# Relation stage: loop over pairs of groups, source-row fills spread over the groups, second bias moved into the relation table

## The chip, the core and the metric

One core of one Trainium2 chip runs the kernel. The metric is the device time of one execution in microseconds. Engines are named as the profile names them: PE (TensorE matmul), PEld (its weight loads), DVE (VectorE), ACT (ScalarE), POOL (GpSimd) and SP (SyncE).

## The reference

Four graph layers run over the same 25,000 edges of a graph with 100,000 nodes of 32 features, each with a residual and a layer norm. The third layer is the one that the change touches:

```python
x = h[src]; y = h[dst]; c = w_comp[etype]
xb = jnp.einsum('ei,bio->ebo', x, weight)          # 16 bases
msg = jnp.einsum('eb,ebo->eo', c, xb)
x_hat = x @ A1_w.T + A1_b
y_hat = y @ A2_w.T + A2_b + rel_emb[etype]
a = jnp.tanh(jax.nn.relu(jnp.sum(x_hat * y_hat, axis=-1) / scale))
nei = segment_sum(a[:, None] * msg, dst)
curr = h[src[last_e]] @ self_loop_weight
h_new = relu(where(in_deg > 0, nei + curr, 0))
```

After it, every node row goes through the last two norms. Rows of nodes that are only sources are written to the output while the relation layer is still being computed, because they get nothing from it.

## The kernel before

The edges lie as 128 partitions by 196 columns (T), so one column is 128 edges. The relation stage takes them in 49 groups (NG) of four columns (GT). Groups are gathered in 7 rounds (ROUNDS) of 7 groups (RG). All engines but SP and POOL walk through the same 49 groups, each in its own program, tied by semaphores. Each group has one of two buffers, b. In the kernel before, b is j % 2, where j is the group's number within its round (0 to 6). So group 6 of a round and group 0 of the next have the same buffer.

For a group g the work is:

- ACT, `stage` (L2262 to L2271): copies the source rows as two half-precision parts (L2268) and the target rows (L2271) into a staging buffer. It does so for group g + 1 ahead of the rest of group g.
- PE, `relation_transpose` (L2559, L2561): transposes group g + 1, into PSUM. In PE's queue this stands ahead of the products of group g.
- ACT: copies group g's transposes out of PSUM (L2321 and L2322), waits until DVE has used group g's linear terms (L2323), and copies the self-loop terms out (L2325).
- PE: the linear products (L2571, L2573, L2575), then the products with the 16 bases, four of 512 columns (L2580), two for each pair of PSUM banks.
- DVE, `relation_groups` (L1988): y_hat plus relation row (L2014), the first two columns' products times the basis weights (L2003, into `prods`), x_hat times y_hat (L2018), the other two columns (L2003, into `nx`), then three sums (L2009, L2025, L2009) and a scale with relu (L2031). Once a round it adds the second bias to the relation rows of that round's 28 columns (L1990).

The rows of plain source nodes leave through a ring of two slots. A slot holds 14 columns (U). ACT scales each column into the slot by an activation (L2332) and copies the 14 indices (L2334). POOL then sends the 14 columns, each by one indirect DMA to the output (`out_src_slot`, L834, L839). ACT fills slots 0 and 1 ahead of the first group, and two more at the end of each of the first six rounds (`out_src_round`, L2336), after waiting for the landing of the slot's earlier contents.

`free(g, j)` gives the count at which a double buffer may be written again. For j = 0 it asks for one group more than elsewhere, because the neighbour has the same buffer. `groups` runs six rounds as a loop, and the last round without a loop.

After the stage DVE multiplies by the tanh, sums over segments and hands a table to SP for writing; POOL then fetches rows of this table (L719, L724).

Of the kernel before, what the change touches and what calls it, by code (L numbers as in the profile page):

```python
# [68 lines left out]
def gnn_resnorm(nc, x, src, dst, etype, eweight, w1, fc_w, fc_b, bias1, w2, w_comp, w_self, A1w, A1b, A2w, A2b,  # L69
# [53 lines left out]
    with ctx:  # L123
# [376 lines left out]

        def free(g, j):


            return g + (CREDIT if j == 0 else CREDIT - 1)

        def groups(eng, body, round_end=None):

            with eng.Fori(0, ROUNDS - 1) as i:
                for j in range(RG):
                    body(i * RG + j, j, False)  # L510
                if round_end:
                    round_end(i)
            for j in range(RG):
                body((ROUNDS - 1) * RG + j, j, j == RG - 1)

# [149 lines left out]
        def _(pool):  # L665
# [167 lines left out]

            def out_src_slot(n, b):  # L834

                pool.wait_ge(s_oslot, n + 1)
                pool.sem_inc(s_tick[0], 1)
                for t in range(U):
                    pool.indirect_dma_start(out=out[:, :], out_offset=bass.IndirectOffsetOnAxis(  # L839
                        ap=oidx[:, b, t:t + 1], axis=0), in_=oring[b][:, t * D:(t + 1) * D], in_offset=None,  # L840
                        bounds_check=N - 1, oob_is_err=False).then_inc(s_oland[b], 16)


            pool.wait_ge(s_nout, 16 * CH)
            with pool.Fori(0, ROUNDS) as k:
                for b in range(2):
                    out_src_slot(k * 2 + b, b)
            pool.wait_ge(s_tabw, 32)
# [8 lines left out]
            for b in range(2):  # L857
                pool.wait_ge(s_oland[b], 16 * U * ROUNDS)
            for h in range(2):
# [6 lines left out]
        def mid(ap, n):  # L866

            return ap.unsqueeze(1).to_broadcast([ap.shape[0], n, ap.shape[1]])

        @block.vector  # L870
        def _(dve):
# [815 lines left out]
            for j in range(GT):  # L1687
# [15 lines left out]
                st.do(V.tensor_copy(bdy[r, j * D:(j + 1) * D], aw[r, D:2 * D]))  # L1703

            st.seq(V.tensor_copy(rel3[:, 0, :], relf[:, :]))
            for k in range(2):
# [280 lines left out]

            def relation_groups(i):  # L1988
                rel = chunk(RB, i, RW)[:, :, NB:RW]
                st.seq(V.tensor_tensor(rel, rel, mid(b_b2[:, :], RC), ALU.add))  # L1990
                pr3 = pr2[:, :].rearrange("p (t o) -> p t o", t=GT)
                pq3 = pq2[:, :].rearrange("p (t o) -> p t o", t=GT)
                for j in range(RG):
                    g, b = i * RG + j, j % 2
                    xh = bank[6 + b][:, 0:256].rearrange("p (t o) -> p t o", t=GT)
                    yh = bank[6 + b][:, 256:256 + P].rearrange("p (t o) -> p t o", t=GT)
                    relg = RB[:, bass.ds(g * (GT * RW), GT * RW)].rearrange("p (t o) -> p t o", t=GT)

                    def basis_mult(c):

                        dve.wait_ge(s_msg, g * GT + (2 * c + 2 + MSG0))
                        dve.sem_inc(tick, 1)
                        st.do(V.tensor_tensor(wide_prods[c].rearrange("p (t o b) -> p t o b", t=2, b=NB),  # L2003
                                              pairs[c][:, :].rearrange("p (t o b) -> p t o b", t=2, b=NB),
                                              relg[:, 2 * c:2 * c + 2, 0:NB].unsqueeze(2).to_broadcast([P, 2, D, NB]),
                                              ALU.mult))

                    def basis_sum(c):
                        st.do(V.tensor_reduce(Y[:, bass.ds(g * (GT * D) + c * 2 * D, 2 * D)],  # L2009
                                              wide_prods[c].rearrange("p (o b) -> p o b", b=NB), AX.X, ALU.add))  # L2010

                    dve.wait_ge(s_xy, g + 1)
                    dve.sem_inc(tick, 1)
                    st.do(V.tensor_tensor(pq3, yh, relg[:, :, NB:RW], ALU.add))  # L2014
                    basis_mult(0)
                    st.wait(1)
                    dve.sem_inc(tick, 1)
                    st.do(V.tensor_tensor(pr3, xh[:, :, 0:D], pq3, ALU.mult))  # L2018
                    st.wait(1)
                    dve.sem_inc(s_msgu, 2)  # L2020
                    basis_mult(1)
                    st.wait(1)
                    dve.sem_inc(s_xyu, 1)
                    basis_sum(0)
                    st.do(V.tensor_reduce(sc4[:, :], pr3, AX.X, ALU.add))  # L2025
                    st.wait(2)
                    dve.sem_inc(s_msgu, 2)
                    basis_sum(1)
                    st.wait(1)
                    dve.sem_inc(tick, 1)  # L2030
                    st.do(V.tensor_scalar(t1[:, bass.ds(g * GT, GT)], sc4[:, :], 1.0 / D ** 0.5, 0.0, ALU.mult, ALU.max))  # L2031

# [3 lines left out]
            dve.wait_ge(s_rcp, NG + 1)  # L2036
            with st.loop(ROUNDS, 1 + 8 * RG) as i:
                relation_groups(i)

# [13 lines left out]
            def table_read():  # L2053
                dve.wait_ge(s_oslot, 2 * ROUNDS)
                dve.wait_ge(s_tabw, 32)
# [63 lines left out]
        def _(act):  # L2119
# [141 lines left out]

            def stage(k, t3_, g, j):  # L2262

                act.wait_ge(s_xtp[k], free(g, j))
                act.sem_inc(tick, 1)
                if k == 1:

                    A.activation(xs16[:, j % 2, :].rearrange("p (t r m) -> p t r m", r=2, m=2 * D),  # L2268
                                 S.bitcast(F16)[:, bass.ds(g * (GT * 2 * D), GT * 2 * D)].rearrange(
                                     "p (t m) -> p t m", m=2 * D).unsqueeze(2).to_broadcast([P, GT, 2, 2 * D]), ACT.Copy)  # L2270
                A.activation(xg[:, j % 2, :].rearrange("p (t d) -> p t d", d=D), edges_g(t3_, g),  # L2271
                             ACT.Copy).then_inc(s_stg[k], 1)

# [37 lines left out]
            act.sem_inc(s_self, CREDIT)  # L2311
            stage(1, XD3, 0, 0)

            def relation_group(g, j, last):
                b = j % 2
                if not last:
                    stage(1, XD3, g + 1, (j + 1) % RG)
                act.wait_ge(s_xtp[1], done(g))
                act.wait_ge(s_msg, free(g, j) * GT)
# [9 lines left out]
            def out_src_fill(slot_, b):  # L2329

                for t in range(U):
                    A.activation(oring[b][:, t * D:(t + 1) * D], XS[:, bass.ds(slot_ * (U * D) + t * D, D)], ACT.Copy,  # L2332
                                 scale=rr[:, bass.ds(slot_ * U + t, 1)])
                A.activation(oidx[:, b, :], osi[:, bass.ds(slot_ * U, U)], ACT.Copy).then_inc(s_oslot, 1)  # L2334
# [9 lines left out]
            groups(act, relation_group, out_src_round)  # L2344
            act.wait_ge(s_ei, 2)
# [4 lines left out]
        def _(pe):  # L2350
# [201 lines left out]

            def relation_transpose(g, j):
                b = j % 2
                pe.wait_ge(s_stg[1], g + 1)
                pe.wait_ge(s_xtc[1], free(g, j))
                pe.sem_inc(tick, 1)
# [4 lines left out]

            def relation_group(g, j, last):
                b = j % 2
                if not last:
                    relation_transpose(g + 1, (j + 1) % RG)
                pe.wait_ge(s_xtc[1], done(g))

                pe.wait_ge(s_self, free(g, j))
                pe.sem_inc(tick, 1)  # L2570
# [42 lines left out]
```

## Time and profile before

| | |
|---|---|
| median of 3 runs | 2988.89 us (2988.18 to 2989.51) |
| the profiled execution | 2987.88 us, its span 2986.1 us |
| busy over the span: DVE | 2053.3 us (69%) |
| POOL | 1783.6 us (60%) |
| ACT | 574.2 us (19%) |
| PE | 536.1 us (18%) |
| relation stage, first to last DVE instruction of the groups | 338.52 us |
| TensorE's granted clock, mean over the stage | 0.57 of full speed |

A granted clock of 0.50 is the lower level (1.2 GHz), 1.00 the higher (2.4 GHz). In the rows of a timeline the first number is the start in microseconds, the second the duration; behind the instruction stands, in square brackets, how long its engine sat idle before it and what ended that. Neighbouring instructions of one engine overlap in part, so the distance between two starts, not the duration, says what an instruction costs its engine.

### The profile page before, as it was taken

How to read it: one execution, taken by the hardware profiler on the slowest of the kernel's cores; microseconds unless marked ns; L12 is line 12 of the kernel's file. 1: busy time of each engine (PE TensorE's matmuls, PEld its weight loads, DVE VectorE, ACT ScalarE, POOL GpSimd, SP SyncE). 2: the span in 40 equal slices, each digit the busy share in tenths (PEclk: the TensorE clock that was granted, in tenths of full speed). 3: DMA queues.
4: the chain of work that ended last, by engine and by line, in shares of the span. 5: the costliest groups of instructions: out<-in, count | busy, mean ns of one | idle time of the engine just before them, and what ended most of it. 6: DMA issues, size and time to landing. Idle time of an engine off the chain costs nothing.

```text
span 2986.1 us, 24643 instructions
## 1 busy us (share of the span) xinstructions
PE 536.1 (18%) x3578; PEld 339.1 (11%) x3578; DVE 2053.3 (69%) x3755; ACT 574.2 (19%) x1342; POOL 1783.6 (60%) x1893
## 2 busy tenths in 40 slices
PE   4760000047100000000003022320245450000000
PEld 2330000036100000000002011220122220000000
DVE  6777878878863555555899377069778788676662
ACT  6970111113000000000012002431233330101000
POOL 5777777777735265556557777670346460715776
PEclk9995555569555555555556555555555555555555
DMA  6002222200011022222120101011000001000000
GB/s 210 13 12 86 76 72 76 66 22 13 12 55 11 20 21 23 26 20 53 55 52 10 52 11 8 1 52 44 4 6 7 6 8 44 10 2 7 10 9 9
DMA packets 78886, 96.54 MB, mean 32 GB/s; under 512 B 45888, under 2 KB 70640, under 8 KB 76920
## 3 DMA queue, kind: packets, MB, share of 16 engines
q0 software_dynamic: 53664, 20.91, 7.0%
q1 hardware_dynamic: 25176, 75.21, 6.7%
q14 instruction: 40, 0.33, 0.0%
q8 instruction: 6, 0.10, 0.0%
HBM read 38.06 MB, written 60.81 MB: 33 GB/s over the span
## 4 chain that ended last, share of the span: by engine, by line
DVE 39%; issue 22%; POOL 13%; DMA 6%; PE 5%; ACT 3%; DVEq 2%; POOLq 1%; ACTq 1%; SPq 0%
POOL ring L724 4%; POOL cring L465 3%; DMA cring<-sums_by_list,cidx 2%; DVE YW L1180 2%; DVE RB L1180 1%; POOL attention_by_edge L820 1%; PE banks L2580 1%; POOL out_dram L481 1%; POOL ring L813 1%; DVE YW L1017 1%; DVE YW L1011 1%; DVE roots L1008 1%; DVE roots L1018 1%; DVE roots L1012 1%; DVE SW L1300 1%
## 5 line engine op out<-in xcount | busy, mean ns | idle before, releaser
L481 POOL DMA_INDIRECT out_dram<-ring,ridx x196 | 206.1, 1051 | 141.5 <-DVE ridx L2074 82.6
L490 POOL DMA_INDIRECT SW<-node_table,srci x196 | 220.8, 1126 | 64.5 <-issue 64.5
L490 POOL DMA_INDIRECT XS<-in_x_dram,xsi x196 | 202.1, 1031 | 81.6 <-issue 62.3
L490 POOL DMA_INDIRECT XD<-in_x_dram,xdi x196 | 202.7, 1034 | 62.6 <-issue 62.6
L839 POOL DMA_INDIRECT out_dram<-z4w,oidx x98 | 96.2, 982 | 225.2 <-ACT oidx L2334 195.6
L465 POOL DMA_INDIRECT cring<-sums_by_list,cidx x128 | 123.6, 966 | 120.4 <-issue 78.8
L2132 ACT ACT_TABLE_LOAD x42 | 53.9, 1283 | 641.6 <-DVEq L997 641.6
L2367 PE MATMUL banks<-YW 128*128 128x392 f16 x784 | 140.2, 333 | 47.5 <-ACT YW L2154 37.6
L2449 PE MATMUL banks<-tl,dcar 128*128 128x32 f32 (+1 forms) x14 | 4.4, 404 | 799.4 <-DVEq L1290 618.3
L724 POOL DMA_INDIRECT ring<-x_by_edge,aidx x96 | 95.1, 990 | 41.9 <-issue 22.5
L942 DVE TENSOR_SCALAR YW<-YW,b_d 128x784 f16<-128x784 f16 x196 | 83.0, 424 | 49.0 <-PE banks L2367 47.1
L839 POOL DMA_INDIRECT out_dram<-e4w,oidx x98 | 96.3, 983 | 29.8 <-issue 29.8
L1180 DVE COPY_PREDICATED YW<-banks,YW 128x2176 f32<-128x2176 int32 (+7 forms) x16 | 95.3, 5959 | 0.5
L2449 PEld LDWEIGHTS banks<-tl,dcar 128*128 128x128 f32 x14 | 3.5, 310 | 801.9 <-DVEq L1290 620.1
L2580 PE MATMUL banks<-w,xw 128*128 128x512 f16 x196 | 93.2, 631 | 0.0
L753 POOL DMA_INDIRECT repeated_edges_by_src<-ring,aidx x64 | 72.2, 1129 | 30.9 <-issue 16.8
L465 POOL DMA_INDIRECT cring<-sums_by_edge,cidx x56 | 52.8, 943 | 62.6 <-DVE cidx L1491 47.8
L2367 PEld LDWEIGHTS banks<-YW 128*128 128x128 f16 x784 | 74.1, 98 | 113.9 <-issue 68.0
L943 DVE TENSOR_SCALAR YW<-YW,b_s 128x784 f16<-128x784 f16 x196 | 82.6, 421 | 0.0
L2427 PE MATMUL banks<-ident,tl 128*128 128x128 f32 x5 | 2.4, 473 | 432.2 <-DVEq L1127 432.2
L2147 ACT ACTIVATE YW<-iota_h,a_d 128x128 f16<-128x128 f16 x196 | 76.4, 390 | 6.1
L2559 PE MATMUL banks<-ident_h,xw 128*128 128x128 f16 x196 | 26.4, 281 | 282.6 <-ACT xg L2271 263.1
(614 smaller groups left out, 3420.8 us busy)
## 6 DMA issues: line engine op xcount, KB each, us to landing
nx<-in_x_dram SPq DMA_DIRECT2D x10, 625.0 KB
YW<-in_x_dram SPq DMA_DIRECT2D x10, 625.0 KB
out_dram<-nx SPq DMA_DIRECT2D x10, 625.0 KB
out_dram<-YW SPq DMA_DIRECT2D x10, 625.0 KB
sums_by_list<-RB SPq DMA_DIRECT2D x2, 1800.0 KB
sums_by_edge<-RB SPq DMA_DIRECT2D x1, 3528.0 KB, 9.8
sums_by_list<-RB SPq DMA_DIRECT2D x2, 1600.0 KB
XS<-in_x_dram,xsi POOLq DMA_INDIRECT x196
```

The lines of the kernel that those rows point to most:

```text
L465: pool.indirect_dma_start(out=row, out_offset=None, in_=table, in_offset=off).then_inc(s_lland[v][h], 16)
L481: pool.indirect_dma_start(out=table, out_offset=off, in_=ring_row(h, j, w), in_offset=None, bounds_check=limit, oob_is_err=False).then_inc ...
L490: pool.indirect_dma_start(out=dest[:, t * w:(t + 1) * w], out_offset=None, in_=table, in_offset=bass.IndirectOffsetOnAxis(ap=idx[:, t:t + ...
L724: pool.indirect_dma_start(out=ring_row(h, j, D), out_offset=None, in_=table, in_offset=bass.IndirectOffsetOnAxis(ap=aidx[:, h, j:j + 1], a ...
L753: pool.indirect_dma_start(out=table, out_offset=bass.IndirectOffsetOnAxis(ap=aidx[:, h, j:j + 1], axis=0), in_=ring_row(h, j, w), in_offse ...
L839: pool.indirect_dma_start(out=out[:, :], out_offset=bass.IndirectOffsetOnAxis(ap=oidx[:, b, t:t + 1], axis=0), in_=oring[b][:, t * D:(t + ...
L942: V.tensor_scalar(oh_lo[0][:, j, :], iota_w, col(b_d), None, ALU.is_equal)
L943: V.tensor_scalar(oh_lo[1][:, j, :], iota_w, col(b_s), None, ALU.is_equal).then_inc(s_oh, 1)
L1180: st.seq(V.copy_predicated(back(t3_[:, n:T, :]), back(bitp[:, n:T].unsqueeze(2).to_broadcast([P, T - n, w])), back(t3_[:, 0:T - n, :])))
L2147: last = A.activation(hi_far[:, j, k * P:(k + 1) * P], iota_h[:, 0:P], ACT.Abs, bias=t[:, bass.ds(i * 4 + j, 1)])
L2367: last = M.matmul(bank[2 * k + h][:, 0:HH], oh_hi[b][:, j, k * P:(k + 1) * P], oh_lo[k][:, j, h * HH:(h + 1) * HH], start=False, stop=False)
L2580: M.matmul(bank[c][:, :], x16[:, b, c * P:(c + 1) * P], w16[:, 0:NB * D], start=True, stop=True).then_inc(s_msg, 1)
```

## The change

1. The relation stage loops over 23 pairs of groups, and the last three groups stand without a loop. The buffer is now the parity of g for all groups, and `free(g)` asks for the same count everywhere.
2. A ring slot holds 4 columns instead of 14. ACT fills slots 0 and 1 ahead of the first group, and slot g + 2 at the end of each group g from 0 to 46, behind the copy of the self-loop terms. POOL sends 49 slots of four columns.
3. The second bias is added once to the small table of relation embeddings (before it is split in three parts), and the addition of 28 columns per round goes.

```diff
-        def free(g, j):
-            return g + (CREDIT if j == 0 else CREDIT - 1)
-        def groups(eng, body, round_end=None):
-            with eng.Fori(0, ROUNDS - 1) as i:
-                for j in range(RG):
-                    body(i * RG + j, j, False)
-                if round_end:
-                    round_end(i)
-            for j in range(RG):
-                body((ROUNDS - 1) * RG + j, j, j == RG - 1)
+        def free(g):
+            return g + (CREDIT - 1)
+        def groups(eng, body):
+            with eng.Fori(0, NG // 2 - 1) as m:
+                for b in range(2):
+                    body(m * 2 + b, b, m)
+            for g in range(NG - 3, NG):
+                body(g, (g - (NG - 3)) % 2, NG // 2 - 1)
...
-            with pool.Fori(0, ROUNDS) as k:
+            with pool.Fori(0, NG // 2) as k:
                 for b in range(2):
-                    out_src_slot(k * 2 + b, b)
+                    out_src_group(k * 2 + b, b)
+            out_src_group(NG - 1, 0)
...
+            st.seq(V.tensor_tensor(relf[:, NB:RW], relf[:, NB:RW], b_b2[:, :], ALU.add))
             st.seq(V.tensor_copy(rel3[:, 0, :], relf[:, :]))
...
-                rel = chunk(RB, i, RW)[:, :, NB:RW]
-                st.seq(V.tensor_tensor(rel, rel, mid(b_b2[:, :], RC), ALU.add))
...
-            with st.loop(ROUNDS, 1 + 8 * RG) as i:
-                relation_groups(i)
+            with st.loop(NG // 2, 2 * 8) as m:
+                for b in range(2):
+                    relation_group(m * 2 + b, b)
+            relation_group(NG - 1, 0)
...
+            def out_src_fill(g, b):
+                for t in range(GT):
+                    A.activation(oring[b][:, t * D:(t + 1) * D], XS[:, bass.ds(g * (GT * D) + t * D, D)], ACT.Copy,
+                                 scale=rr[:, bass.ds(g * GT + t, 1)])
+                A.activation(oidx[:, b, 0:GT], osi[:, bass.ds(g * GT, GT)], ACT.Copy).then_inc(s_oslot, 1)
...
                              ACT.Copy).then_inc(s_self, 1)
-            def out_src_round(i):
-                for b in range(2):
-                    act.wait_ge(s_oland[b], i * (16 * U) + 16 * U)
+                if more(2):
+                    act.wait_ge(s_oland[b], m * (16 * GT) + 16 * GT)
                     act.sem_inc(tick, 1)
-                    out_src_fill(i * 2 + (2 + b), b)
+                    out_src_fill(g + 2, b)
```

## Rows read from the trace of the kernel before

**Rows 1.** Busy time by windows: round 1, then the stage; PE, PEld, DVE, ACT, POOL, clock.

```profile
2187.23:2236.81 49.58, 24.52 (x114) 12.84 (x113) 38.75 (x57) 18.03 (x65) 27.50 (x28) 0.53 0.03 6
2137.18:2475.70 338.52, 166.79 (x767) 86.19 (x765) 270.19 (x399) 118.89 (x420) 188.61 (x192) 0.57 0.04 7
```

**Rows 2.** Waits of the stage (2136 to 2476): total us, times, longest.

```profile
ACT SW L2325 <- DVEq L2023: 218.4, 49, 5.0
DVE prods L2003 <- PE banks L2580: 22.5, 46, 0.5
```

**Rows 3.** Timeline of a steady group, the steps of its cycle only.

```profile
2406.04 1.23 DVE L2003 TENSOR_TENSOR nx<-banks,RB 128x1024 f32<-128x1024 f32 x1 [0.23 <-DVE pr L2018]
2406.36 0.28 ACT L2325 ACTIVATE SW<-banks 128x128 f32 x1 [4.38 <-DVEq L2023]
2406.55 0.63 ACT L2268 ACTIVATE xw<-SW 128x512 f16 x1
...
2407.76 0.27 ACT L2322 ACTIVATE xt<-banks 128x128 f32<-128x128 f32 x1
...
2409.14 1.91 PE L2580 MATMUL banks<-w,xw 128*128 128x512 f16 x4
...
2410.44 1.23 DVE L2003 TENSOR_TENSOR prods<-banks,RB 128x1024 f32<-128x1024 f32 x1 [0.46 <-PE banks L2580]
...
2412.42 0.28 ACT L2325 ACTIVATE SW<-banks 128x128 f32 x1 [4.39 <-DVEq L2023]
```

**Rows 4.** Timeline of a round's end, with the two fills of 14 columns.

```profile
2425.22 0.28 ACT L2325 ACTIVATE SW<-banks 128x128 f32 x1 [5.03 <-DVEq L2023]
2425.60 3.08 ACT L2332 ACTIVATE z4w<-XS,c 128x32 f32 x14
...
2428.55 1.08 DVE L1990 TENSOR_TENSOR RB<-RB,b_b 128x896 f32 x1
2428.58 0.20 ACT L2334 ACTIVATE oidx<-xsi 128x14 int32 x1
...
2431.76 0.61 ACT L2268 ACTIVATE xw<-SW 128x512 f16<-128x512 f16 x1
...
2434.79 0.29 DVE L2014 TENSOR_TENSOR pq<-banks,RB 128x128 f32<-128x128 f32 x1 [5.16 <-PE banks L2575]
```

**Rows 5.** Timeline of the group before it, whose neighbour shares the buffer.

```profile
2418.47 0.28 ACT L2325 ACTIVATE SW<-banks 128x128 f32 x1 [4.39 <-DVEq L2023]
...
2420.34 0.59 PE L2559 MATMUL banks<-ident_h,xw 128*128 128x128 f16 x4 [3.24 <-ACT xt L2322]
```

**Rows 6.** Timeline ahead of the first group: the first two slots.

```profile
2128.01 3.06 ACT L2332 ACTIVATE z4w<-XS,c 128x32 f32<-128x32 f32 x14
...
2132.06 0.98 POOL L839 DMA_INDIRECT out_dram<-z4w,oidx  x1 [114.29 <-ACT oidx L2334]
2133.34 0.98 POOL L839 DMA_INDIRECT out_dram<-z4w,oidx  x1 [0.30 <-issue]
...
2134.15 0.61 ACT L2268 ACTIVATE xw<-SW 128x512 f16 x1
```

**Rows 7.** All of line 839: from issue to landing.

```profile
DMA to landing us min/median/max: 2.1/2.1/3.3
```

**Rows 8.** Timeline of DVE where the relation table is split.

```profile
993.02 0.21 DVE L1707 TENSOR_TENSOR relf<-relf,rel 128x48 f32<-128x48 f32 x1
```

**Rows 9.** Timeline at a jump back of ACT's loop, between its last and first instruction.

```profile
2184.09 0.20 ACT L2334 ACTIVATE oidx<-xsi 128x14 int32 x1
2184.19 0.61 ACT L2268 ACTIVATE xw<-SW 128x512 f16 x1
```

**Rows 10.** Timeline of a group of the last round that met the higher clock.

```profile
2462.57 0.28 ACT L2322 ACTIVATE xt<-banks 128x128 f32<-128x128 f32 x1
...
2463.52 0.62 PE L2580 MATMUL banks<-w,xw 128*128 128x512 f16 x1
```

**Rows 11.** Timeline after the stage: POOL's first work after its last scatter.

```profile
2533.18 0.19 POOL L719 COPY aidx<-rows 128x4 int32<-128x4 int32 x1 [67.78 <-DMA rgcn_table<-SW]
```

More of the change, by code:

```diff
@@ L832, in _, with out_src_group @@
             put_rows(ns, qi, SA, D, att_d[:, :], s_dset, s_dput, EP - 1)
-            def out_src_slot(n, b):
+            def out_src_group(n, b):
                 pool.wait_ge(s_oslot, n + 1)
                 pool.sem_inc(s_tick[0], 1)
-                for t in range(U):
+                for t in range(GT):
                     pool.indirect_dma_start(out=out[:, :], out_offset=bass.IndirectOffsetOnAxis(
@@ L857, in _ @@
             for b in range(2):
[L858 removed]
+                pool.wait_ge(s_oland[b], 16 * GT * ((NG + 1 - b) // 2))
             for h in range(2):
@@ L1986, in _, with relation_group @@
             norm_run(XS, sq_2, add_bias(XS, Y), parts16, both=True)
-            def relation_groups(i):
-                rel = chunk(RB, i, RW)[:, :, NB:RW]
-                st.seq(V.tensor_tensor(rel, rel, mid(b_b2[:, :], RC), ALU.add))
+            def relation_group(g, b):
                 pr3 = pr2[:, :].rearrange("p (t o) -> p t o", t=GT)
                 pq3 = pq2[:, :].rearrange("p (t o) -> p t o", t=GT)
[L1993 to L2012, printed above, removed]
-                    dve.sem_inc(tick, 1)
[L2014 to L2031, printed above, removed]
@@ new lines, in relation_group, with basis_mult @@
+                xh = bank[6 + b][:, 0:256].rearrange("p (t o) -> p t o", t=GT)
+                yh = bank[6 + b][:, 256:256 + P].rearrange("p (t o) -> p t o", t=GT)
+                relg = RB[:, bass.ds(g * (GT * RW), GT * RW)].rearrange("p (t o) -> p t o", t=GT)
+                def basis_mult(c):
+                    dve.wait_ge(s_msg, g * GT + (2 * c + 2 + MSG0))
+                    dve.sem_inc(tick, 1)
+                    st.do(V.tensor_tensor(wide_prods[c].rearrange("p (t o b) -> p t o b", t=2, b=NB),
+                                          pairs[c][:, :].rearrange("p (t o b) -> p t o b", t=2, b=NB),
+                                          relg[:, 2 * c:2 * c + 2, 0:NB].unsqueeze(2).to_broadcast([P, 2, D, NB]),
+                                          ALU.mult))
@@ new lines, in basis_sum @@
+                def basis_sum(c):
+                    st.do(V.tensor_reduce(Y[:, bass.ds(g * (GT * D) + c * 2 * D, 2 * D)],
+                                          wide_prods[c].rearrange("p (o b) -> p o b", b=NB), AX.X, ALU.add))
+                dve.wait_ge(s_xy, g + 1)
+                dve.sem_inc(tick, 1)
+                st.do(V.tensor_tensor(pq3, yh, relg[:, :, NB:RW], ALU.add))
+                basis_mult(0)
+                st.wait(1)
+                dve.sem_inc(tick, 1)
+                st.do(V.tensor_tensor(pr3, xh[:, :, 0:D], pq3, ALU.mult))
@@ new lines, in relation_group @@
+                st.wait(1)
+                dve.sem_inc(s_msgu, 2)
+                basis_mult(1)
+                st.wait(1)
+                dve.sem_inc(s_xyu, 1)
+                basis_sum(0)
+                st.do(V.tensor_reduce(sc4[:, :], pr3, AX.X, ALU.add))
+                st.wait(2)
+                dve.sem_inc(s_msgu, 2)
+                basis_sum(1)
+                st.wait(1)
+                dve.sem_inc(tick, 1)
+                st.do(V.tensor_scalar(t1[:, bass.ds(g * GT, GT)], sc4[:, :], 1.0 / D ** 0.5, 0.0, ALU.mult, ALU.max))
@@ L2053, in table_read @@
             def table_read():
-                dve.wait_ge(s_oslot, 2 * ROUNDS)
+                dve.wait_ge(s_oslot, NG)
                 dve.wait_ge(s_tabw, 32)
@@ L2260, in _, with stage @@
             edges_g = lambda t3_, g: t3_[:, bass.ds(g * GT, GT), 0:D]
-            def stage(k, t3_, g, j):
-                act.wait_ge(s_xtp[k], free(g, j))
+            def stage(g, b):
+                act.wait_ge(s_xtp[1], free(g))
                 act.sem_inc(tick, 1)
[L2266 to L2272, printed above, removed]
+                A.activation(xs16[:, b, :].rearrange("p (t r m) -> p t r m", r=2, m=2 * D),
+                             S.bitcast(F16)[:, bass.ds(g * (GT * 2 * D), GT * 2 * D)].rearrange(
+                                 "p (t m) -> p t m", m=2 * D).unsqueeze(2).to_broadcast([P, GT, 2, 2 * D]), ACT.Copy)
+                A.activation(xg[:, b, :].rearrange("p (t d) -> p t d", d=D), edges_g(XD3, g),
+                             ACT.Copy).then_inc(s_stg[1], 1)
             act.wait_ge(s_ei, 1)
@@ L2311, in _, with relation_group @@
             act.sem_inc(s_self, CREDIT)
[L2312 to L2317, printed above, removed]
+            stage(0, 0)
+            def out_src_fill(g, b):
+                for t in range(GT):
+                    A.activation(oring[b][:, t * D:(t + 1) * D], XS[:, bass.ds(g * (GT * D) + t * D, D)], ACT.Copy,
+                                 scale=rr[:, bass.ds(g * GT + t, 1)])
+                A.activation(oidx[:, b, 0:GT], osi[:, bass.ds(g * GT, GT)], ACT.Copy).then_inc(s_oslot, 1)
+            def relation_group(g, b, m):
+                more = lambda n: not isinstance(g, int) or g + n < NG
+                if more(1):
+                    stage(g + 1, 1 - b)
                 act.wait_ge(s_xtp[1], done(g))
-                act.wait_ge(s_msg, free(g, j) * GT)
+                act.wait_ge(s_msg, free(g) * GT)
                 act.sem_inc(tick, 1)
@@ L2327, in relation_group @@
                              ACT.Copy).then_inc(s_self, 1)
[L2329 to L2334, printed above, removed]
-            def out_src_round(i):
-                for b in range(2):
-                    act.wait_ge(s_oland[b], i * (16 * U) + 16 * U)
+                if more(2):
+                    act.wait_ge(s_oland[b], m * (16 * GT) + 16 * GT)
                     act.sem_inc(tick, 1)
-                    out_src_fill(i * 2 + (2 + b), b)
+                    out_src_fill(g + 2, b)
             for b in range(2):
                 out_src_fill(b, b)
-            groups(act, relation_group, out_src_round)
+            groups(act, relation_group)
             act.wait_ge(s_ei, 2)
@@ L2551, in _, with relation_transpose @@
             pe.sem_inc(s_msg, MSG0)
-            def relation_transpose(g, j):
-                b = j % 2
+            def relation_transpose(g, b):
                 pe.wait_ge(s_stg[1], g + 1)
-                pe.wait_ge(s_xtc[1], free(g, j))
+                pe.wait_ge(s_xtc[1], free(g))
                 pe.sem_inc(tick, 1)
@@ L2561, in relation_transpose, with relation_group @@
                 M.transpose(bank[4 + b][:, 256:256 + P], xg[:, b, :], ident[:, :]).then_inc(s_xtp[1], 1)
[L2563 to L2566, printed above, removed]
+            def relation_group(g, b, m):
+                if not isinstance(g, int) or g + 1 < NG:
+                    relation_transpose(g + 1, 1 - b)
                 pe.wait_ge(s_xtc[1], done(g))
-                pe.wait_ge(s_self, free(g, j))
+                pe.wait_ge(s_self, free(g))
                 pe.sem_inc(tick, 1)
```

## The prediction

> **What bounds the kernel now.** I read in this order: the page's slices and groups, to find where line 839 and its neighbours run; the busy time of that stretch; its waits; then one steady group, one round's end and the start of the stage instruction by instruction. The page's chain is of no use here: it runs over POOL's last scatters, though POOL then waits 67.8 us for the table that comes out of the stage [rows 11]. What ends the stage is therefore DVE's last group, and all behind it moves with it.
>
> The stage takes 338.5 us from DVE's first to its last instruction, for 49 groups. DVE is busy 270 of them, ACT only 119 [rows 1]. ACT sits idle 218.4 us at one wait, once in each of the 49 groups: it waits for DVE to have used the linear terms. DVE in turn waits for the basis products in 46 of 49 groups, 22.5 us in all [rows 2]. Two engines that both wait for each other in every group are in a cycle, and the cycle sets the pace, not the busy time.
>
> The steady group shows the cycle [rows 3]. DVE starts `nx` at 2406.04 and with that lets ACT go. ACT copies the self-loop terms at 2406.36 (+0.32), stages the group after next at 2406.55 (+0.19), and copies the transposes of the next group, the second one at 2407.76 (+1.21). PE waits for both: for the staged rows, since their transposes stand ahead in its queue, and for the copies. It starts the basis products at 2409.14 (+1.38). DVE starts `prods` when two of them are out, at 2410.44 (+1.30), after 0.46 us of waiting. The next self-loop copy starts at 2412.42 (+1.98), which is 6.06 us behind the one before. I take 6.05. Anything put on ACT between the self-loop copy and the staging lengthens this cycle by its whole length, although ACT is idle for 4.4 us of every group.
>
> **The change part by part.**
>
> (a) The fills leave the round's end. A round's end is a test of that last sentence, made by the kernel before itself: there, two fills stand just behind the self-loop copy. From that copy (2425.22) to the first fill are 0.38 us, where a steady group has 0.19 to the staging; the 14 columns take 2.98 us to the index copy (2428.58), 0.213 us a column; from the first fill to the staging at 2431.76 are 6.16 us for two fills, so an index copy is (6.16 - 2 x 2.98) / 2 = 0.10 [rows 3, 4]. The extra is 0.19 + 6.16 = 6.35 us. DVE gets its next linear terms at 2434.79, after 5.16 us of idling [rows 4]. All of the 6.35 is on the path. Six round ends: -38.1 us.
>
> (b) The shared buffer at each round's end. The group before it takes from 2418.47 to 2425.22, 6.75 us instead of 6.05, because PE's transposes (2420.34) wait for ACT's copy out of the same buffer instead of for the staging [rows 4, 5]. True parity takes this away: 6 x 0.70 = -4.2 us.
>
> (c) The fills come back, one in each group. `out_src_fill(g + 2)` stands behind the self-loop copy of group g and ahead of the next group's staging, the very place of (a). It costs 0.19 for the way into it, 4 x 0.213 = 0.85 for four columns and 0.10 for the indices [rows 3, 4]: 1.14 us. 47 groups have one (0 to 46): +53.6 us. The columns are the same 196 in both kernels and all stood on the path before, too; what is new is 35 more index copies (49 for 14) and 41 more ways in (47 for 6), 3.5 + 7.8 = 11.3 us. The bounds: below, the way in costs nothing more than the 0.19 that the staging had, 0.95 a group; above, ACT's queue of instructions is only four or five ahead in place of 28, so that address arithmetic and the jump back show, for which I allow 0.25 more, 1.40 a group. That is +44.7 to +65.8 us. I take 1.14, since the round's end is the same code in the same place.
>
> (d) The start. Ahead of the first group ACT fills both slots, 2128.01 to 2134.15, 6.14 us, before it stages group 1 [rows 6]. Now they are 2 x (0.85 + 0.10) = 1.90. -4.2 us.
>
> (e) The ring's waits. In a steady group the fill of slot g + 2 waits for the landing of slot g, filled two groups earlier, some 2 x 7.2 - 1.0 = 13.4 us ago. POOL began 1.1 us behind the index copy before (2132.06; the copy stood at about 2128.01 + 6.14 / 2 - 0.10 = 2130.98), sends a column each 1.28 us and a column lands in 2.1 to 3.3 us [rows 6, 7]: 1.1 + 3 x 1.28 + 3.3 = 8.2 us. No wait. POOL's own 5.1 us a slot lie under 7.2. Only at the first group is it close: slot 0 is sent from about 2130.0 and landed at 2136 to 2137, and ACT wants it at 2136.2. I take +0.4, bounds 0 and 0.9.
>
> (f) The second bias. The seven additions of 1.08 us stand at the start of each round, under DVE's idle time of 5.16 us [rows 4], and in the first round under the wait for ACT's first fills. Taking them away gives nothing; without that cover they would have cost 7.6 us. In their place stands one small addition behind which DVE waits, at the splitting of the table, where such a one lies 0.24 us ahead of the next instruction [rows 8]: +0.2. DVE is the busy engine there, so it counts.
>
> (g) The loops. There are 23 jumps back on each engine instead of 6. At a jump back of ACT's loop the staging starts 0.10 us behind the index copy [rows 9], no more than an index copy costs inside. PE and DVE jump while they wait for others. I take 0. By the Trainium skill (Advanced Engine Details and Errata, Control Flow Timing) an unconditional branch takes about 51 ns and a compare-and-branch about 108 ns. An estimate from that page, were both in full view at the 17 additional jumps, would be 2.7 us more, and the sum below +10.4 instead of +7.7; the trace's row speaks for the lower, as long as ACT's queue is ahead.
>
> Sum: -38.1 - 4.2 + 53.6 - 4.2 + 0.4 + 0.2 = +7.7 us. As a check by rounds: an undisturbed round takes 49.58 us [rows 1]; without its end and its shared buffer 42.5, with seven fills 50.5. Each of six rounds grows by 0.9 us, and the last, which had no fills and now has five, by 5.7; less the 4.2 of the start and plus the 0.6 of (e) and (f), that is again +7.7. The profiled execution took 2987.88 us and would take 2995.6; the median of the runs shown is 1.0 us above it, so I forecast **2996.6 us**.
>
> **The rivals.**
>
> Hidden fills (faster). ACT idles 4.4 us a group, five times what a fill needs. If the fill ran in that idle time, the cycle would stay at 6.05, and only the savings would count: -38.1 - 4.2 - 4.2 + 0.6 = -45.9, 2943 us. It decides by the place: it holds if ACT can begin the fill while the self-loop copy still waits. The order in the code and the round's end, where all 28 columns came out of the path's time, speak against it.
>
> Higher clock (faster). PE ran the stage mostly at the lower level (mean 0.57) [rows 1]. In one group of the last round that met the higher level, the way from the second copy (2462.57) to the basis products (2463.52) was 0.95 instead of 1.38 [rows 3, 10], and two products of 512 columns, 0.43 us each at the lower level as four in 1.91 us with the last of 0.62 show, could take half. That is 0.43 + 0.43 = 0.86 less a group, -41 in all, 2956 us. The pause of PE in each group grows by the fill's 1.14 us, and its busy share falls from 0.49 of a round [rows 1] to 0.48, so nothing speaks for a higher clock than before. By the Trainium skill (TensorE: Matmul & The Clock Gate, Part 1) the throttled clock is the default and activity releases it; by that rule the longer pause keeps the clock low, and the sum stands.
>
> Cheap fills (no change). With 0.95 a group, the lower bound of (c), the sum is -1.2: 2987.7 us. It decides by the distance from the self-loop copy to the first fill.
>
> Ring bound (slower). If a slot's four columns took over 13 us from fill to landing, ACT would wait for the landing in each group, with PE and DVE behind it. At 16 us the two-slot ring gives a group each 8.5 us or so, 1.3 more in 47 groups: +69, 3058 us. Rows 6 and 7 speak for 8.2 us.
>
> Parity without effect: if the transposes still wait for the copy, 4.2 us stay: 3001 us.
>
> **How the numbers follow.** About 0.2% (6 us) is what a measurement of this kernel can tell from no change, so 2983 to 2995 is the same. Sum within its bounds: 0.83, of which fills of up to 1.10 us a group (the sum below +6) have 0.20 and dearer ones 0.63. Hidden fills 0.07, higher clock 0.05, ring 0.02, parity without effect 0.03. Faster 0.12, same 0.20, slower 0.68. The bounds of (c) put the sum at -1.2 to +19.9, with (e) +0.5: 2987.5 to 3009.5. What is left out is the two faster rivals, the ring and the last of the dear end, just under 2 in 10: the range is 2987 to 3009.
>
> **What would show it.** Right: self-loop copies 7.1 to 7.3 us apart in all groups but the last, with no long gap; the first fill 0.38 behind the self-loop copy; ACT's wait at that copy still near 4.4 us; POOL without waits on landings but idle about 2 us for each slot; the stage about 8 us longer from the first copy. Wrong: distances near 6.05 (hidden), distances near 6.3 with a clock near 1.00, a wait of ACT ahead of line 2332 (ring), a gap between the index copy and the staging at each second group (jumps).

## The result, and the profile after

The changed kernel takes 2998.81 us (2997.36 to 2999.67, 8 runs), the kernel before beside it 2989.08 us (8 runs): 1.0033 times as long, 95% interval 1.0022 to 1.0044, or 9.7 us more (6.6 to 13.2). The forecast was 7.7 us more.

The stage by windows, from DVE's first to its last instruction of the groups (length, then busy time and count of PE, PEld, DVE, ACT and POOL, the granted clock, DMA share and GB/s), and the stage's waits (total us, times, longest), both of the changed kernel:

```profile
2134.11:2486.00 351.89, 171.12 (x767) 88.62 (x765) 267.11 (x392) 130.41 (x475) 190.16 (x194) 0.57 0.03 7
```

```profile
ACT SW L2329 <- DVEq L2019: 217.1, 49, 4.5
...
DVE pq L2010 <- PE banks L2568: 54.0, 48, 6.3
...
DVE prods L1999 <- PE banks L2573: 25.9, 48, 0.5
```

The stage is 351.89 us long instead of 338.52 [rows 1]; it begins relatively earlier (below), so its end moved by 10.3 us. ACT still idles 217 us at the self-loop copy, once in each of the 49 groups, as before [rows 2]. The clock is the same 0.57. DVE now waits for the linear terms in 48 groups, 54.0 us. In the kernel before it waited for them in 13, at the start and around the rounds' ends, as the same view of that kernel has it:

```profile
DVE pq L2014 <- PE banks L2575: 42.9, 13, 8.8
```

ACT's timeline over two groups of the changed kernel (start, duration; in brackets the idle time ahead):

```profile
2296.78 0.28 ACT L2329 ACTIVATE SW<-banks 128x128 f32 x1 [4.49 <-DVEq L2019]
2297.08 0.96 ACT L2313 ACTIVATE z4w<-XS,c 128x32 f32 x4
2297.95 0.19 ACT L2315 ACTIVATE oidx<-xsi 128x4 int32 x1
2298.04 0.61 ACT L2264 ACTIVATE xw<-SW 128x512 f16 x1
...
2303.88 0.28 ACT L2329 ACTIVATE SW<-banks 128x128 f32 x1 [4.39 <-DVEq L2019]
2304.11 0.96 ACT L2313 ACTIVATE e4w<-XS,c 128x32 f32 x4
2304.98 0.19 ACT L2315 ACTIVATE oidx<-xsi 128x4 int32 x1
2305.31 0.63 ACT L2264 ACTIVATE xw<-SW 128x512 f16 x1
...
2311.28 0.28 ACT L2329 ACTIVATE SW<-banks 128x128 f32 x1 [4.49 <-DVEq L2019]
```

The first fill uses `z4w`, slot 0, the second `e4w`, slot 1, the last of the loop's body. Self-loop copies are 7.10 us apart inside a pair and 7.40 across the jump back; but for 7.70 at the first jump back, this pattern holds within 0.04 us for all 45 distances inside the loop. The last three, behind the loop, are 6.96, 6.89 and 5.25 us. From self-loop copy to staging are 1.26 us and 1.43 us, where a steady group of the kernel before has 0.19 [rows 3]. Across the jump, 0.33 lie between index copy and staging instead of 0.09, and PE begins its products (L2564) 0.50 instead of 0.40 behind the copy of the transposes (L2326).

The start of the stage, timeline of the changed kernel:

```profile
2129.10 0.94 ACT L2313 ACTIVATE z4w<-XS,c 128x32 f32<-128x32 f32 x4
...
2130.98 0.61 ACT L2264 ACTIVATE xw<-SW 128x512 f16 x1
2131.02 0.98 POOL L836 DMA_INDIRECT out_dram<-z4w,oidx  x1 [112.06 <-ACT oidx L2315]
...
2136.92 0.28 ACT L2329 ACTIVATE SW<-banks 128x128 f32 x1 [4.48 <-DVEq L2019]
2137.24 0.96 ACT L2313 ACTIVATE z4w<-XS,c 128x32 f32 x4
```

Two slots take 1.88 us instead of 6.14 [rows 6]. The third fill starts 0.32 behind the first self-loop copy, like all others of its kind: it waits for no landing.

### The profile page after: what moved, and what is told of

Read it like the earlier page. It is cut to its first block, busy times and chain, and to the rows that moved or that the text cites. A ratio compares the mean times of both kernels' runs of the same rounds, so it can differ in the third digit from the quotient of the medians.

```text
span 2997.2 us, 25018 instructions
## 1 busy us (share of the span) xinstructions
PE 539.4 (18%) x3578; PEld 341.3 (11%) x3578; DVE 2051.0 (68%) x3749; ACT 581.6 (19%) x1377; POOL 1784.3 (60%) x1893
## 4 chain that ended last, share of the span: by engine, by line
DVE 39%; issue 22%; POOL 13%; DMA 6%; PE 5%; ACT 3%; DVEq 2%; ACTq 1%; POOLq 1%; SPq 0%
POOL ring L721 4%; POOL cring L465 3%; DMA cring<-sums_by_list,cidx 2%; DVE YW L1178 2%; DVE RB L1178 1%; POOL attention_by_edge L817 1%; PE banks L2573 1%; POOL ring L810 1%; POOL out_dram L481 1%; DVE YW L1015 1%; DVE YW L1009 1%; DVE roots L1016 1%; DVE roots L1006 1%; DVE roots L1010 1%; DVE SW L1298 1%
## 5 line engine op out<-in xcount | busy, mean ns | idle before, releaser
L1999 DVE TENSOR_TENSOR prods<-banks,RB 128x1024 f32<-128x1024 f32 x49 | 60.0, 1225 | 25.9 <-PE banks L2573 25.9
```

## The experiments

In all of them the spacing of the self-loop copies is the measure of a group, and the kernel before ran beside them as the reference. The "cycle theory" of the expectations is the prediction's: an instruction of ACT costs in full between the self-loop copy and the copies of the transposes, and nothing while ACT would otherwise wait for DVE. Parts of the code that stand still are marked by `...`.

### The fill in ACT's idle time

```diff
                 A.activation(xt[:, b, :], bank[4 + b][:, 256:256 + P], ACT.Copy).then_inc(s_xtc[1], 1)
+                if more(2):
+                    act.wait_ge(s_oland[b], m * (16 * GT) + 16 * GT)
+                    act.sem_inc(tick, 1)
+                    out_src_fill(g + 2, b)
                 act.wait_ge(s_xyu, done(g))
...
-                if more(2):
-                    act.wait_ge(s_oland[b], m * (16 * GT) + 16 * GT)
-                    act.sem_inc(tick, 1)
-                    out_src_fill(g + 2, b)
```

> The changed kernel with one edit: ACT's fill of slot g + 2 stands ahead of its wait for DVE and of the self-loop copy, behind the copies of the transposes, and no longer between the self-loop copy and the next staging. Work and order of the slots are the same. Cycle theory (ACT's instructions cost in full between self-loop copy and staging, and nothing in its idle 4.4 us): self-loop copies 6.05 us apart inside a pair and some 6.3 across a jump back, the stage 47 x 1.0 us shorter than in the changed kernel, 2998.8 - 48 = 2951 us, ACT's wait at the self-loop copy 1.0 us shorter. Rival (a fill of four columns costs wherever it stands, through the ring's landings, POOL or the larger number of instructions): 7.1 and 7.4 us as before, 2999 us.

Measured: 2956.95 us, 0.9894 of the kernel before (0.9878 to 0.9909). ACT's timeline over two groups of idle_fill:

```profile
2303.72 0.28 ACT L2333 ACTIVATE SW<-banks 128x128 f32 x1 [3.56 <-DVEq L2019]
2303.91 0.63 ACT L2264 ACTIVATE xw<-SW 128x512 f16 x1
...
2305.28 0.95 ACT L2313 ACTIVATE e4w<-XS,c 128x32 f32 x4
2306.13 0.20 ACT L2315 ACTIVATE oidx<-xsi 128x4 int32 x1
2309.85 0.28 ACT L2333 ACTIVATE SW<-banks 128x128 f32 x1 [3.53 <-DVEq L2019]
2310.45 0.63 ACT L2264 ACTIVATE xw<-SW 128x512 f16 x1 [0.32 <-issue]
```

Groups take 6.13 us inside a pair. The same fill now fills idle time: ACT's wait is 3.5 us instead of 4.4. The cycle theory holds, the rival falls. But across the jump a group takes 6.57: the staging starts 0.60 behind the self-loop copy instead of 0.19, with 0.32 of pure issue; these 0.41 are more than the 0.24 that the jump costs ACT in the changed kernel. I had expected 6.3 there, which is 22 x 0.27 = 6 us too little; the groups inside a pair are 0.08 longer than expected (their self-loop copy starts 0.40 behind `nx` instead of 0.33), another 1.8 us. And the first fill of the loop now comes too early for the ring, as this row shows:

```profile
2137.60 0.96 ACT L2313 ACTIVATE z4w<-XS,c 128x32 f32 x4 [4.80 <-DMA out_dram<-z4w,oidx]
```

It waits for the landing of slot 0, and so the first self-loop copy starts 1.3 us later than it would behind DVE alone (1.61 behind `nx` instead of 0.33). Against that, each fill was worth a little more than the 1.0 us of the expectation (1.05 in the changed kernel); together the time lies 6 us above it.

### Twice the columns, in the path and beside it

```diff
+                for t in range(GT):
+                    A.activation((z4w, e4w)[b][:, U * D + t * D:U * D + (t + 1) * D], XS[:, bass.ds(g * (GT * D) + t * D, D)],
+                                 ACT.Copy, scale=rr[:, bass.ds(g * GT + t, 1)])
                 A.activation(oidx[:, b, 0:GT], osi[:, bass.ds(g * GT, GT)], ACT.Copy).then_inc(s_oslot, 1)
```

> The changed kernel with four more scaled column copies (into unused columns of the same tile) in each fill, at the same place between self-loop copy and staging; 0.86 us of additional ACT work a group. Cycle theory: all of it is on the path, self-loop copies 7.96 and 8.26 us apart, 47 x 0.86 + 1.7 for the first two slots = +42, 3041 us. Rival (the fill costs by its fixed parts, such as waits and index copy, or through POOL, and columns are cheap): under +10 us.

> The kernel idle_fill (2957 us) with the same four more column copies in each fill, which there stands in ACT's idle time. Cycle theory: +1.7 us for the two slots ahead of the first group and nothing else, 2958.7 us; ACT's wait at the self-loop copy falls from 3.5 to 2.6 us a group. If ACT's busy time or port counts for itself: up to +40, 2997 us.

Measured: 3036.12 us for double_fill, 37.3 us above the changed kernel; 2956.56 us for idle_double, the same as idle_fill (2.1 us under its expectation: the two longer slots at the start do put the first self-loop copy 1.0 us later, but groups inside a pair take 6.07 instead of 6.13 us, as their self-loop copy starts 0.33 behind `nx` instead of 0.40; why it does, no run shows). ACT's timelines, double_fill across a jump, then idle_double:

```profile
2243.57 0.28 ACT L2332 ACTIVATE SW<-banks 128x128 f32 x1 [4.45 <-DVEq L2019]
2243.80 0.96 ACT L2313 ACTIVATE e4w<-XS,c 128x32 f32 x4
2244.66 0.94 ACT L2316 ACTIVATE e4w<-XS,c 128x32 f32 x4
2245.51 0.19 ACT L2318 ACTIVATE oidx<-xsi 128x4 int32 x1
2245.61 0.61 ACT L2264 ACTIVATE xw<-SW 128x512 f16 x1
```

```profile
2303.82 0.28 ACT L2336 ACTIVATE SW<-banks 128x128 f32 x1 [2.71 <-DVEq L2019]
...
2305.39 0.95 ACT L2313 ACTIVATE e4w<-XS,c 128x32 f32 x4
2306.24 0.95 ACT L2316 ACTIVATE e4w<-XS,c 128x32 f32 x4
```

The same four columns are worth 37 us at one place and nothing at the other, where ACT's wait only shrinks to 2.7 us. In double_fill nearly all groups take 7.97 to 8.02 us: those inside a pair grew by 0.92 (0.06 of it because their self-loop copy starts 0.40 behind `nx` instead of 0.33), those across the jump only by 0.57, because there the staging now starts 0.10 behind the index copy instead of 0.33. Behind the nine instructions of the doubled fill the jump is hidden, behind the five of the single one it is not. They have to stand behind ACT's wait for DVE: idle_double has the same nine ahead of that wait, and across its jump the staging still starts 0.60 behind the self-loop copy. 22 x 0.29 less 23 x 0.06 = 5 us is what the measured time lies below the expectation.

### Longer loops

```diff
-            with eng.Fori(0, NG // 2 - 1) as m:
-                for b in range(2):
-                    body(m * 2 + b, b, m)
-            for g in range(NG - 3, NG):
-                body(g, (g - (NG - 3)) % 2, NG // 2 - 1)
+            with eng.Fori(0, NG // 14) as q:
+                for k in range(14):
+                    body(q * 14 + k, k % 2, q * 7 + k // 2)
+            for g in range(NG - 7, NG):
+                body(g, g % 2, g // 2)
```

(and the same for DVE's loop)

> The changed kernel with one edit: the three compute engines loop over 14 groups (three rounds, then seven groups without a loop) instead of over pairs, so 2 jumps back each instead of 22; fills, buffers and order are the same. In the changed kernel self-loop copies are 7.10 us apart within a pair and 7.40 across the jump. If the 0.30 is the jump's (0.24 between ACT's index copy and its next staging, 0.10 on PE, less 0.05), all groups come to about 7.1: 20 x 0.30 = 6 us less, 2993 us. If it hangs on the buffer or slot of odd groups, 7.10 and 7.40 alternate on, 2999 us.

Measured: 2993.57 us, 1.0018 of the kernel before (1.0009 to 1.0027). The groups inside the loop take 7.09 and 7.02 us in turn: the 0.30 is the jump's and not the slot's. But the sum agrees with the expectation by errors against each other: the two jumps back cost 5.2 us together, the seven groups at the end give 2.6 back, and every second group is 0.08 shorter than expected. ACT's timeline at one of the two jumps back of long_loop:

```profile
2230.26 0.19 ACT L2316 ACTIVATE oidx<-xsi 128x4 int32 x1
2232.74 0.63 ACT L2265 ACTIVATE xw<-SW 128x512 f16 x1 [2.29 <-issue]
```

A jump over 14 groups of code costs 2.3 us on ACT (groups of 9.54 and 9.71 us). The page's row of the queue that loads instructions (packets, MB, share) points at the reason; long_loop, then the changed kernel:

```profile
q14 instruction: 63, 0.52, 0.1%
```

```profile
q14 instruction: 37, 0.30, 0.0%
```

That is 26 more loads of code over the whole run. They lie in the stage (2100 to 2500: 28 packets against 3) and come back with each pass of the loop: 7 from 2215 to 2255, around the first jump back. At each of the two jumps one starts inside ACT's gap (from 2230 to 2231, and from 2332 to 2333). The changed kernel has a single packet from 2170 to 2475, with some 20 jumps. So the long loop's code is loaded again in each pass. For which engine a packet is, the trace does not say. parity_only, below, has a loop of 14 groups too, 64 packets over the run, and the same gap at its jump, there behind two fills of 14 columns:

```profile
2232.95 0.20 ACT L2337 ACTIVATE oidx<-xsi 128x14 int32 x1
2234.47 0.63 ACT L2271 ACTIVATE xw<-SW 128x512 f16 x1 [1.32 <-issue]
```

So this stall, unlike the 0.24 us of the short jump, isn't fully hidden by the work ahead of it. On the other side, the seven groups at the end of long_loop, written out with constant addresses, take mostly 6.55 us. The clock isn't the reason, since it was lower there (0.50, last figure but two) than over the end of the loop (0.66):

```profile
2387.00:2429.70 42.70, 20.90 (x98) 11.30 (x97) 32.97 (x49) 16.08 (x60) 23.86 (x25) 0.66 0.04 7
2429.70:2470.50 40.80, 21.77 (x99) 11.30 (x97) 32.98 (x50) 15.51 (x60) 23.92 (x25) 0.50 0.04 8
```

### One part at a time, in the kernel before

```diff
+            st.seq(V.tensor_tensor(relf[:, NB:RW], relf[:, NB:RW], b_b2[:, :], ALU.add))
             st.seq(V.tensor_copy(rel3[:, 0, :], relf[:, :]))
...
-                rel = chunk(RB, i, RW)[:, :, NB:RW]
-                st.seq(V.tensor_tensor(rel, rel, mid(b_b2[:, :], RC), ALU.add))
```

> The kernel before with the third part of the change alone: the second bias is added to the small table, and the seven additions of 28 columns go. If they are hidden under DVE's wait for ACT's fills: +0.2 us for the new small addition, nothing back, 2989.1 against 2988.9 (same). If they were on the path: -7.6 + 0.2, 2981.5 us.

```diff
-            return g + (CREDIT if j == 0 else CREDIT - 1)
+            return g + (CREDIT - 1)
...
+            with eng.Fori(0, (ROUNDS - 1) // 2) as q:
+                for r in range(2):
+                    for j in range(RG):
+                        body(q * (2 * RG) + (r * RG + j), r * RG + j, False)
+                    if round_end:
+                        round_end(q * 2 + r)
```

(and the same for DVE's loop, with the parity of g as the buffer)

> The kernel before with true buffer parity alone: the loop goes over two rounds of seven groups at a time, a group's buffer is g % 2, and no group waits for one more than the others; the two fills of 14 columns stay at each round's end, the bias additions stay. Six groups of 6.75 us become 6.05: -4.2 us, 2984.8 us. If the wait moves elsewhere: unchanged, 2989 us.

Measured: 2988.89 us for bias_only, 1.0001 (0.9992 to 1.0010), and 2986.18 us for parity_only, 0.9991 (0.9982 to 1.0000). The bias additions were hidden. In parity_only the groups ahead of a round's end take 6.05 instead of 6.75, as forecast. Of the 4.2 us only 2.4 arrive in the time. The sum is a mixed one: its loop is 14 groups long, and the two round ends with a jump take 13.9 us instead of 12.4, 3.0 us in all; against that, its last six distances are 5.3 to 5.6 us instead of 5.5 to 6.1, 1.8 us in all, since DVE's last round stands without a loop as well. So parity's worth is shown by the groups and not by the time.

### ACT's jump in idle time

```diff
-            groups(act, relation_group)
+            stage(1, 1)
+            copies(0, 0)
+            groups(act, relation_group)
```

Here `relation_group(g)` is cut anew: fill of slot g + 2, wait and self-loop copy of g, `stage(g + 2)`, `copies(g + 1)` (lines 2325 and 2326 of the changed kernel with their waits).

> The kernel idle_fill with ACT's loop cut at another point: its body now goes from the fill to the copies of the next group's transposes, so that the jump back stands ahead of ACT's idle time; order of all ACT instructions unchanged. There, ACT's staging starts 0.60 behind the self-loop copy across a jump and 0.19 elsewhere. If the jump is exposed only in the cycle: 0.19 everywhere, groups of 6.14 and 6.16 us, 22 x 0.41 = 9.0 us less than idle_fill, 2948 us. If a jump costs its time wherever it stands: unchanged, 2957 us.

Measured: 2947.48 us, 0.9863 (0.9846 to 0.9879), 9.5 us less than idle_fill. ACT's timeline of rotated, two groups:

```profile
2305.29 0.28 ACT L2334 ACTIVATE SW<-banks 128x128 f32 x1 [3.47 <-DVEq L2019]
2305.56 0.63 ACT L2264 ACTIVATE xw<-SW 128x512 f16 x1
...
2311.53 0.28 ACT L2334 ACTIVATE SW<-banks 128x128 f32 x1 [3.55 <-DVEq L2019]
2311.72 0.63 ACT L2264 ACTIVATE xw<-SW 128x512 f16 x1
```

The order of ACT's instructions is the same as in idle_fill; only the place of the jump differs. The staging follows 0.27 and 0.19 behind the self-loop copy, the groups take 6.24 and 6.08 us. Of ACT's 0.41 us, 0.08 are left; the rest of the difference between the two groups is PE's, whose jump was not moved: its products still begin 0.50 instead of 0.41 behind the copy of the transposes. A jump, too, costs only where it stands in the cycle.

### All groups written out

```diff
-            with eng.Fori(0, NG // 2 - 1) as m:
...
+            for g in range(NG):
+                body(g, g % 2, g // 2)
...
-            for b in range(2):
-                out_src_fill(b, b)
...
+                if not isinstance(g, int) or g > 1:
+                    act.wait_ge(s_oland[b], m * (16 * GT))
+                    act.sem_inc(tick, 1)
+                out_src_fill(g, b)
                 act.wait_ge(s_xyu, done(g))
```

> The changed kernel with fills in ACT's idle time, those of slots 0 and 1 too, and all 49 groups of ACT, PE and DVE written out without a loop, with constant addresses. In the seven groups without a loop at the end of long_loop the steps with addresses from registers were shorter (self-loop copy 0.17 behind nx instead of 0.33, nx 1.49 behind prods instead of 1.65) and a group took 6.55 instead of 7.05. Taking the in-path fill's 1.03 away leaves 5.5 to 5.65 a group, near the 5.3 of DVE alone: 48 x 5.6 = 269 us against 302.5, and 1.9 us less at the start, 2921 us. If fetching long straight code holds the engines up (the first groups of a loop took up to 0.35 more each), 6.0 to 6.3 a group: 2940 to 2955 us.

Measured: 2917.41 us, 0.9762 of the kernel before (0.9746 to 0.9779), the fastest of all here. DVE and ACT in one group of unrolled:

```profile
2301.66 1.22 DVE L1996 TENSOR_TENSOR prods<-banks,RB 128x1024 f32<-128x1024 f32 x1 [0.20 <-PE banks L2566]
2302.80 0.28 DVE L2011 TENSOR_TENSOR pr<-banks,pq 128x128 f32<-128x128 f32 x1
2303.14 1.23 DVE L1996 TENSOR_TENSOR nx<-banks,RB 128x1024 f32<-128x1024 f32 x1
2303.32 0.28 ACT L2328 ACTIVATE SW<-banks 128x128 f32<-128x128 f32 x1 [3.05 <-DVEq L2016]
...
2307.28 1.23 DVE L1996 TENSOR_TENSOR prods<-banks,RB 128x1024 f32<-128x1024 f32 x1 [0.21 <-PE banks L2566]
```

A group takes 5.62 us, or 5.3 to 5.5 in about one of three, where DVE waits for nothing. This run changes three things at once: the fills' place, the jumps and the addresses. The part of the addresses is seen in single steps. `nx` starts 1.65 behind `prods` in every group in which DVE is in a loop, and 1.48 where it is written out (here, and in the last groups of long_loop and parity_only). The self-loop copy starts 0.33 behind `nx` where both engines are in loops [rows 3 have 0.32], 0.25 where ACT alone is written out (near the end of the changed kernel and in the last round of the kernel before), and 0.18 where both are. The straight code stalls nothing that shows: no group is longer than 5.63 us.

## Why the prediction was right

**What was called.** The prediction has the right direction, the right mechanism for its largest terms, and a time 2.2 us below the measured one. But its own signs, listed ahead of the result, are mixed. Right: ACT's wait stayed at 4.4 us, no fill waits for a landing, POOL idles 2.4 us for each slot, and from the first copy of a fill to the last self-loop copy it is 9.2 us longer, for about 8. Wrong: the distances across a jump are 7.40 and not 7.1 to 7.3, the first fill starts 0.30 or 0.23 behind the self-loop copy and not 0.38, and the gap between index copy and staging at each second group is there. Without the jumps, which it took at nothing, the sum with the measured fills would have been +3.1 us, which the prediction counts as no change. That it came out slower by its own measure (over 6 us) is owed to a term that stands in its sum with 0, and in its range only as part of the 0.25 us by which a fill might be dearer.

**What bounds the kernel.** The cycle through ACT, PE and DVE, with ACT idle in every group, is shown by idle_fill, double_fill and idle_double: one and the same edit is worth 0 or 0.9 us a group by its place.

**(a), (b), (d), (f), by their working.** The rounds' ends are gone: the six distances with two fills of 14 columns come to 37.9 us more than six steady ones, for 38.1. True parity gives 0.70 a round (parity_only). The first two slots take 1.88 us instead of 6.14, -4.3 for -4.2. The bias additions were hidden (bias_only), and the new small one starts 0.23 us ahead of the next instruction in the changed kernel, for +0.2.

**(c), the fills.** I took 1.14 us. Inside a pair it is 7.10 - 6.05 = 1.05: four columns and indices as forecast, but the way in from the self-loop copy is 0.30 us, or 0.23, where 14 columns after a round had 0.38. That is 47 x 0.09 = 4.2 us too much.

**(g), the jumps.** This is the step that was wrong. I took 0 for the jumps because the row at a jump back showed 0.10 us [rows 9]. That row stands behind 28 columns of ACT work, and I had named the condition ("as long as ACT's queue is ahead") without pricing it from this kernel. With the five instructions of a fill ahead, the jump shows with 0.24 us on ACT and 0.10 on PE, less 0.07 for a shorter way in; the distances themselves differ by 0.30: 22 x 0.30 = 6.6 us. That PE jumps while it waits did not spare it the 0.10. In long_loop PE's 0.10 appears in the first group of each pass and nowhere else, which ties it to the loop. Since the very first group has it as well, and the kernel before has it in none, whether it is the jump itself or work at the head of the body stays open. double_fill hides ACT's part again, and rotated, in the other place, leaves 0.08 of the 0.41 that idle_fill has. The Trainium skill's figures (Advanced Engine Details and Errata, Control Flow Timing: about 51 ns for an unconditional branch, about 108 ns for a compare-and-branch) add up to an estimate of 0.16 us a jump. The trace has 0.24 on ACT behind the five instructions of a fill and 0.41 behind the self-loop copy alone: here the measurement decides, and the two branches by themselves are too little for what a loop's jump costs this engine.

**(e), the ring.** The first landing cost nothing, for +0.4; no fill waits anywhere in the changed kernel. That it was close shows in idle_fill, where the first fill comes earlier and waits.

Together: -4.2 + 6.6 - 0.4 = +2.0 us on top of 7.7, which is the measured 9.7. The agreement to a tenth is chance. In the profiled executions, 2997.2 and 2986.1 us of span, the difference is 11.1 us, and it falls apart thus: the 48 distances between self-loop copies sum to 345.6 us instead of 332.2, 13.4 more, where the terms that lie in them, (a), (b), (c) and (e), had 11.7; the start gives 4.2 back, as forecast; 1.1 us lie ahead of the stage (ACT's first staging of the stage begins at 2128.36 instead of 2127.27), where the change adds 0.2, and 0.8 behind it. Those two are not the change's as far as is known: in bias_only and parity_only the same staging begins at 2128.85 and 2128.96, so executions differ there by that much. Within the 13.4, the four terms by their measured sizes give 13.9 (-37.9 - 4.2 + 49.4 + 6.6). The rest of -0.5 is small things that the prediction did not have: the second group of each round took about 0.2 us more (0.65 in the first round), which is gone; the last round stood without a loop and was cheaper, of which only three groups are left.

Two small slips of the working change nothing: PE's busy share would have fallen to 0.486, not 0.48 (the stage has 0.486), and the lower bounds of (c) and (e) together give 2987.3, not 2987.5.

**The rivals.** Hidden fills were not what this kernel does, but idle_fill shows that the mechanism and its price were right: 2957 us measured, 2943 by the rival, with 9.5 us of the difference in jumps (rotated), 1.3 in the first fill's wait for its slot, and the rest in groups that are some 0.08 longer than 6.05. Higher clock: the clock stayed at 0.57, and even unrolled has only 0.61 over its stage; what the higher clock would be worth, no run tests. Cheap fills: 1.05 us lies midway between the 0.95 of that rival and the 1.14 of the sum, and it was the jumps that kept the sum from being no change. Ring bound: no fill of the changed kernel waits for a landing. Parity without effect: refuted by the groups of parity_only.

## What to carry to other kernels

In a pipeline where engines wait for each other in turn, find the cycle and note for each engine which stretch of its queue lies on it; work put between "let go by the other" and "hand over to the next" costs in full, even on an engine that is idle most of the time, and the same work ahead of its wait costs nothing. Spreading a lump of work evenly doesn't help if each piece lands in that stretch and adds its own fixed costs. The same holds for a loop's jump: cut the body so that the jump stands ahead of the engine's longest wait, or write the stage out. What failed here was the way between the two, a loop with a body of 14 groups: it had few jumps, but a stall at each.

## What the runs showed of the hardware

- A jump back costs ACT 0.41 us behind the one instruction that follows its wait (idle_fill, and idle_double), 0.24 behind the five of a fill (the changed kernel), and nothing that shows behind nine or more (double_fill, and [rows 9]). PE loses 0.10 us in the first group of each pass of its loop (the changed kernel, long_loop, rotated, parity_only), but not in the kernel before.
- A loop over 14 groups of code stalls ACT at its jump, 2.29 and 2.46 us behind a fill of four columns (long_loop) and 1.32 us behind two of 14 (parity_only). The instruction queue's packets over the run are 63 and 64 there, and 37 to 47 in all other kernels. They come back in each pass of the loop. The loop over 7 groups of the kernel before has one packet from 2195 to 2435 and no stall at its jumps [rows 9]; straight code of 49 groups has 13 packets in its stage and no stall that shows.
- Constant addresses in place of register arithmetic shortened a group's cycle by about 0.5 us (long_loop: from 7.05 in the loop to 6.55 behind it, at the lower clock): 0.17 between `prods` and `nx`, some 0.15 from `nx` to the self-loop copy, the rest spread.
- ACT's column copies of 128 x 32 elements are 0.21 to 0.22 us apart whether a piece has 4 or 14 of them; the fixed price of a piece was 0.2 us in the changed kernel (its index copy and its way in).
